# Decoder block: the cross attention of sequence 0 moved into the second self-attention pass, and what moves with it

## The reference

```python
x = x + attn(layernorm(x))            # 16 heads of 128, biases on q, k, v and the output
x = x + xattn(layernorm(x), ctx, ctx) # 8 heads of 64 rows; the q is the sequence's 64x512 row block
x = x + ffn(layernorm(x))             # w2q @ (silu(x w1q) * (x w3q)), 1365 hidden, ternary weights
```

## Time and profile before

| | us |
|---|---|
| median of 3 runs | 1212.6 (1211.21 to 1213.02) |
| the profiled execution, its own time | 1214.28 |
| its span, first to last instruction | 1212.4 |
| PE busy | 1135.5 (94%) |
| DVE, ACT, POOL busy | 755.4, 551.7, 448.4 |

### The profile page before, as it was taken

How to read it: one execution, slowest core, us unless ns; L and a number is a source line. 1 busy time by engine, 2 the same in 40 slices (tenths; PEclk the granted TensorE clock), 3 DMA queues, 4 the chain that set the end, 5 groups by cost and what they waited for, 6 DMA issues and landing times.

```text
span 1212.4 us, 16525 instructions
## 1 busy us (share of the span) xinstructions
PE 1135.5 (94%) x5792; PEld 946.3 (78%) x5792; DVE 755.4 (62%) x1401; ACT 551.7 (46%) x1145; POOL 448.4 (37%) x388
## 2 busy tenths in 40 slices
PE   5999997999999999999999978779998999999997
PEld 3888885878788888888888856568877887888786
DVE  7555459797465655353232478878866886787531
ACT  2455672324151244562332237657727762875230
POOL 2222328041341123380403036546625661674030
PEclk9999999899999999999999979979999999999999
DMA  7455553455302143411200143922203110410000
GB/s 225 132 184 183 188 180 122 162 173 175 110 19 87 52 152 127 148 43 62 70 1 1 44 147 101 309 79 70 62 27 114 61 44 35 122 45 1 35 1 35
DMA packets 52789, 118.99 MB, mean 98 GB/s; under 512 B 9977, under 2 KB 9977, under 8 KB 50666
## 3 DMA queue, kind: packets, MB, share of 16 engines
q1 hardware_dynamic: 52714, 118.03, 30.4%
HBM read 101.22 MB, written 16.79 MB: 97 GB/s over the span
## 4 chain that ended last, share of the span: by engine, by line
PE 80%; DVE 10%; ACT 4%; issue 3%; POOL 2%; DMA 1%; SPq 0%; POOLq 0%; ACTq 0%; DVEq 0%
PE bank L102 16%; PE bank L103 16%; PE bank L104 16%; PE bank L441 6%; PE bank L442 6%; PE bank L405 4%; PE bank L453 3%; PE bank L454 3%; PE bank L415 2%; PE bank L427 2%; PE bank L416 2%; PE bank L428 2%; DVE pxl L615 1%; POOL wal L1415 1%; DVE wlow L1367 1%
## 5 line engine op out<-in xcount | busy, mean ns | idle before, releaser
L441 PE MATMUL bank<-x3h,w 128*128 128x512 f32 (+1 forms) x352 | 141.8, 403 | 1.6 <-DVE x3l L689 1.6
L442 PE MATMUL bank<-x3l,w 128*128 128x512 f32 (+1 forms) x352 | 139.1, 395 | 0.0
L769 POOL TENSOR_SCALAR pe_x<-pe_x,xri,gam 128x512 f32<-128x512 f32 x128 | 101.7, 795 | 100.6 <-DVE xri L624 94.6
L1074 ACT ACTIVATE yh<-bank 128x512 fp32r<-128x512 f32 x64 | 37.9, 601 | 219.8 <-PE bank L104 219.7
L1415 POOL TENSOR_TENSOR wal<-raw_a,wah 128x512 fp32r<-128x512 f32 x44 | 62.3, 1446 | 201.2 <-ACT wah L1095 201.2
L102 PE MATMUL bank<-yh,rh 128*128 128x512 f32 x256 | 101.6, 397 | 10.4 <-DVE xacc L1301 10.4
L535 ACT ACTIVATE pe_x<-bank,xmx 128x512 f32<-128x512 f32 x128 | 88.0, 687 | 40.8 <-DVE xmx L620 39.6
L1232 DVE TENSOR_TENSOR ml<-bank,mh 128x512 fp32r<-128x512 f32 x64 | 43.5, 690 | 100.0 <-ACT mh L1074 100.0
L1420 POOL TENSOR_TENSOR wbl<-raw_b,wbh 128x512 fp32r<-128x512 f32 x64 | 87.8, 1406 | 45.1 <-ACT wbh L1113 45.1
L1232 DVE TENSOR_TENSOR yl<-bank,yh 128x512 fp32r<-128x512 f32 x64 | 43.8, 690 | 96.9 <-ACT yh L1074 96.9
L620 DVE TENSOR_REDUCE xmx<-bank 128x1 f32<-128x512 f32 x128 | 87.3, 682 | 26.5 <-PE bank L416 23.2
(11 more groups left out here) (137 smaller groups left out, 2939.9 us busy)
## 6 DMA issues: line engine op xcount, KB each, us to landing
raw_a<-in_wk SPq DMA_DIRECT2D x8, 1024.0 KB, 5.3
raw_b<-in_wq SPq DMA_DIRECT2D x8, 1024.0 KB, 5.3
raw_a<-in_wo SPq DMA_DIRECT2D x8, 1024.0 KB, 5.5
raw_b<-in_wvt SPq DMA_DIRECT2D x8, 1024.0 KB, 4.9
x1d<-x_scratch SPq DMA_DIRECT2D x64, 128.0 KB, 3.2
kd<-in_ctx SPq DMA_DIRECT2D x64, 128.0 KB, 3.2
ternary_scratch<-wraw SPq DMA_DIRECT2D x24, 341.2 KB, 3.0
w<-ternary_scratch SPq DMA_DIRECT2D x2, 2730.0 KB
```

The costliest lines, as they stand in the source:

```text
L441: pe.matmul(u_bank[w][0:m, :], lhs, x3h[:, c, :], start=c == 0, stop=False)
L442: mm = pe.matmul(u_bank[w][0:m, :], lhs, x3l[:, c, :], start=False, stop=c == CK - 1)
L769: pool.tensor_scalar(pe_x[:, q, :], pe_x[:, q, :], xri[:, q:q + 1], gam[:], ALU.mult, ALU.mult).then_inc(s["xpn"], 1)
```

## The change

Turn 0 is gone. Its 32 steps and the tail of its last head are done inside the second pass: steps between and inside the M tiles of the scores (nine steps for each group of eight tiles, the first of them in the fifth tile of group 0), the tail in the first Y tiles of the values. `early` names a set of tiles for it that lies in memory then free, with one PSUM bank for scores, one for transposes and one for results, where `main` has two, two and one. The M ring has three banks for this part in place of four. The biases of the q weights are added on POOL (`pool_add`) and not on DVE. `xacc` for the second pass is loaded only when the steps are over, since their tiles lie there. The x2 of sequence 0 goes to DRAM and comes back late in the values; its layer norm and transposes lie among the last outputs. W1 is loaded in the values' first group, W3 before the last group, W2 at the start of turn 1. The moments of sequence 3 are formed in the first four steps of turn 1. Turns 1, 2, 3 and the last are all written out, with no loop on any engine.

```diff
+PLACES = (0, 1, 2, 3, 4, 5, 8, 6, 7)
+def early_step(g, place):
+    n = len(PLACES) * g - 4 + PLACES.index(place)
+    return n if n >= 0 else None
...
+        early = Mem(
...
+            s=[bank[6]] * 2, t=[bank[7]] * 2, r=bank[3], ring=1)
...
-        def turns(engine_loop, body):
-            body(0, None, 1)
-            with engine_loop(1, B - 1) as b:
-                body(b, b - 1, b + 1)
-            body(B - 1, B - 2, None)
+        def turns(body):
+            for b in range(1, B):
+                body(b, b - 1, b + 1 if b + 1 < B else None)
             body(None, B - 1, None)
...
+        def sp_w2(sp):
+            sp.wait_ge(s["out_ready"], PASSES * GROUPS * PB * HG)
+            for b in range(B - PB, B):
+                sp.wait_ge(s[f"x1_out{b}"], 16)
...
+        def sp_w13(sp, w):
+            if w == 0:
+                sp.wait_ge(s["a_ready"], A["M", PASSES - 1, GROUPS - 1, CK - 1, PB - 1] + 1)
...
+            else:
+                sp.wait_ge(s["wal_pool"], wal_pool(PASSES, 0))
+                sp.wait_ge(s["wbl"], CK * load(PASSES, 0))
+            sp.dma_start(w13[:, w].bitcast(F32), wq_dram[w].rearrange("(c p) n -> p c n", p=P)).then_inc(s["w_in"], 16)
...
+        def sp_early_start(sp):
+            sp.wait_ge(s["x1_out0"], 16)
+            sp.wait_ge(s["st_out0"], 16)
+            sp_stats(sp, 0)
+            sp_head(sp, early, 0, 0)
+            sp_head(sp, early, 0, 1)
+            sp.dma_start(early.x2[:], x1_dram[0].rearrange("(t p) c -> p t c", p=P)).then_inc(s["x2_in"], 16)
...
+        def sp_early_end(sp):
+            sp.wait_ge(s["r_free"], XH)
+            sp.dma_start(x1_dram[0].rearrange("(t p) c -> p t c", p=P), early.x2[:]).then_inc(s["x2_out"], 16)
...
+        def sp_scores_early(sp):
+            p = PASSES - 1
+            sp_x1_data(sp, p - 1, 0)
+            sp_x1_stat(sp, p - 1, 0)
+            sp_x1_data(sp, p - 1, 1)
+            for g in range(GROUPS):
+                sp_slot_a(sp, p, g + 1)
+                if g + 1 < GROUPS:
+                    sp.wait_ge(s["wadd_b"], wadd_b(p, g + 1))
+                    sp_row(sp, wk, bk, g + 1)
+                if g == 0:
+                    sp_early_start(sp)
+                    sp_slot_b(sp, p, g + 1)
+                    sp_x1_stat(sp, p - 1, 1)
+                    sp_head(sp, early, 0, 2)
+                    sp_head(sp, early, 0, 3)
+                elif g == 1:
+                    sp_head(sp, early, 0, 4)
+                    sp_slot_b(sp, p, g + 1)
+                    sp_head(sp, early, 0, 5)
+                elif g == 2:
+                    sp_head(sp, early, 0, 6)
+                    sp_head(sp, early, 0, 7)
+                    sp_slot_b(sp, p, g + 1)
+                else:
+                    sp_slot_b(sp, p, g + 1)
+                if g + 1 < GROUPS:
+                    sp.wait_ge(s["wadd_a"], wadd_a(p, g + 2))
+                    sp_row(sp, wq, bq, g + 1)
...
+        def pe_t_early(pe, g, pr, before):
+            p = PASSES - 1
+            pe.wait_ge(s["s_read"], pair(p, g, pr) + 1)
+            pe.wait_ge(s["t_free"], before)
...
+        def pe_early_scores(pe, n):
+            h, q = divmod(n, 4)
+            if n == 0:
+                pe.wait_ge(s["out_free"], out_index(PASSES - 2, GROUPS - 1, PB - 1, HG - 1) + 1)
+            pe_sx(pe, early, 0, h, q)
+            if n == 0:
+                pe_vt(pe, early, 0, 0)
+            elif n % 8 == 7 and h + 1 < XH:
+                pe_vt(pe, early, 0, h + 1)
+            if q == 1 and h >= 2:
+                pe_ret(pe, early, 0, h - 2, 1)
+            if q == 3 and h >= 1:
+                pe_ret(pe, early, 0, h - 1, 0)
...
+        def pe_early_turn(pe, n):
+            h, q = divmod(n, 4)
+            if h:
+                pe_pt(pe, early, 0, h - 1, q)
...
+        def pe_scores_early(pe):
+            p = PASSES - 1
+            for g in range(GROUPS):
+                for place in range(2 * CK):
+                    c, i = divmod(place, PB)
+                    n = early_step(g, place)
+                    pe_m_tile(pe, p, g, c, i, range(0, CK // 2))
+                    if n is not None:
+                        if g and place == 4:
+                            pe.wait_ge(s["att_free"], pair(p, g - 1, 0) + 1)
+                        if g and place == 7:
+                            pe.wait_ge(s["att_free"], pair(p, g - 1, 1) + 1)
+                        pe_early_turn(pe, n)
+                    pe_m_tile(pe, p, g, c, i, range(CK // 2, CK))
+                    if n is not None:
+                        pe_early_scores(pe, n)
+                    if place == 3:
+                        pe_s(pe, p, g, 0)
+                        if g:
+                            pe_t_early(pe, g - 1, 0, tiles_before(early_step(g, 4)))
+                    if place == 5:
+                        pe_s(pe, p, g, 1)
+                        pe_early_turn(pe, early_step(g, 8))
+                        pe_early_scores(pe, early_step(g, 8))
+                    if place == 6 and g:
+                        pe_t_early(pe, g - 1, 1, tiles_before(early_step(g, 7)))
+                    if place == 7:
+                        pe_s(pe, p, g, 2)
+                        pe_s(pe, p, g, 3)
...
+        def pe_y_early(pe):
+            last = XH - 1
+            for c in range(CK):
+                pe_y_tile(pe, PASSES - 1, 0, 0, c, range(0, TJ // 2))
+                if c == 0:
...
+                if c == 1:
...
+                pe_y_tile(pe, PASSES - 1, 0, 0, c, range(TJ // 2, TJ))
...
+                act_vt(act, early, 0, h + 1)
+            act_exp(act, early, 0, h, q)
+            if q == 0 and h + 1 < XH:
+                act_prep(act, early, 0, h + 1)
...
+        def act_scores_early(act):
+            p = PASSES - 1
+            for g in range(GROUPS):
+                for place in range(2 * CK):
+                    c, i = divmod(place, PB)
+                    if early_step(g, place) is not None:
+                        act_early_rows(act, early_step(g, place))
+                    act_high(act, mh[:, c % 2, i, :], A["M", p, g, c, i])
+                    if g and 1 <= place <= CK:
+                        act_split_b(act, p, g, [place - 1])
+                    if place == 2 * CK - 1:
+                        act_split_a(act, p, g + 1, range(0, 2))
+                    if early_step(g, place) is not None:
+                        act_early_step(act, early_step(g, place))
+                    if place == 0 and g:
+                        act_attention_half(act, p, g - 1, 1)
+                    if place == 3:
+                        if g:
+                            act_t_half(act, p, g - 1, 0, early.t[0])
+                        else:
+                            act_prep(act, early, 0, 0)
+                    if place == 5:
+                        if g == GROUPS - 1:
+                            act_matrix(act, p, 0)
+                        act_early_rows(act, early_step(g, 8))
+                        act_early_step(act, early_step(g, 8))
+                    if place == 6 and g:
+                        act_t_half(act, p, g - 1, 1, early.t[0])
+                act_split_a(act, p, g + 1, range(2, CK))
+                if g == GROUPS - 1:
+                    act_bias_v(act, p, g + 1)
+                act_attention_half(act, p, g, 0)
...
+        def dve_early_rows(dve, n):
+            h, q = divmod(n, 4)
+            if h:
+                dve_px(dve, early, 0, h - 1, q)
+            if n:
+                dve_rinv(dve, early, 0, (n - 1) // 4, (n - 1) % 4)
...
+        def dve_scores_early(dve, link):
+            p = PASSES - 1
+            for g in range(GROUPS):
+                for place in range(2 * CK):
+                    c, i = divmod(place, PB)
+                    n = early_step(g, place)
+                    if n is not None:
+                        dve_early_rows(dve, n)
+                        dve_early_max(dve, n)
+                    dve_low(dve, ml[:, c % 2, i, :], mh[:, c % 2, i, :], A["M", p, g, c, i])
+                    if n is not None:
+                        dve_early_values(dve, n)
+                    if g == 0 and place < 4:
+                        dve_x1(dve, link, p - 1, 1, place)
+                    if g == 0 and place == 3:
+                        dve_q(dve, early, 0, 0)
+                    if place == 1 and g:
+                        dve_shares(dve, p, g - 1)
+                    if g + 1 < GROUPS:
+                        if place == 2:
+                            dve_row(dve, link, p, g + 1, "a")
+                        if 3 <= place < 3 + CK:
+                            dve_add(dve, p, g + 1, "a", place - 3)
+                        if place == 2 * CK - 1:
+                            dve_row(dve, link, p, g + 1, "b")
+                            dve.sem_inc(s["row_sum"], 1)
+                    elif place == 2 * CK - 1:
+                        dve_bias_v(dve, p, 0)
+                    if place == 5:
```

(32 more changed lines are left out.)

801 lines of the change are left out of this document (487 added, 314 removed).

## The result

Median 1200.4 us (1199.7 to 1203.5, 4 runs) against 1212.8 for the kernel before, a ratio of 0.9907 (0.9893 to 0.9921): 11 us less, or 12.4 by the medians. The forecast was 1183, 29.4 less on the profiled execution's own time. The direction held, and so did the range, whose upper end is 1201, by less than 1 us; more than half of the gain did not come. The profiled execution took 1199.98 us, with a span of 1198.2. All ratios here are of runs in the chip's usual, faster state; the one run outside it (1295.1 us, of the loop alone) is left out.

What follows compares the result with a forecast made beforehand. PE was taken as the bound, unfilled only in turn 0. Removing 97.7 us less 52.8 of replacing work gives 44.9, plus 2.1 for the loop, minus 17.6 of waits: 29.4 less, so 1183 us, range 1170 to 1201.

Steps and rivals of the forecast that it cites:

- rival 3: Clock falls after PE waits near 2.84 us, at the steps' start and turn 1's start: five holes cost 8 us, 1191; chance 0.10.
- (a): First step in group 0 of the second pass's scores: PE waits for DVE, ACT and POOL; net 1.5 us, between 0 and 5.
- (b): Between score groups: `wah` and `wal` come late behind the inserted work; stalls of 5.6 us, between 1 and 12.
- (c): Self-attention transposes share the one transpose bank: PE waits for ACT's copy 0.5 us six times, 3 in all, 0 to 6.
- (d): Layer norm of sequence 0 on DVE before the first of the last outputs: PE waits about 1.5 us, 0 to 4.
- (e): Tail of the moved work in the Y tiles: 1 us of waits, 0 to 3.
- (f): Moments of sequence 3 in turn 1's first four steps delay DVE's maxima and the exponentials: 5 us, between 2 and 8.
- The loop: Turn 2 written out instead of entered over the loop's back edge should be like turn 3: 2.1 us gained.
- Rival 1: Everything fits: waits of 5 us in all in place of 17.6, giving 1171; chance 0.12.
- Rival 2: The single score bank binds: 1.1 us more for each of 32 steps, giving 1208; chance 0.11.
- Rival 4: DVE operations lose time to POOL on the shared port: 12 us more at a whole POOL operation each, 1195; chance 0.06.
- Rival 5: Bias rows come late to DVE six times in the second pass: at 7 us late each, 1225; chance 0.06.

Runs made afterwards that it cites:

- the filled waits: Changed kernel with matmuls nobody reads put into three PE waits (16 before the first step, 11 before the third output, 12 before the last turn's first `pe_down`): 1194.9 us, 0.9868.
- the three tries: Changed kernel with first-step loads reordered: two heads' context first, 1199.7 us; head 0's only, DVE's subtraction ahead of sequence 1's chain, 1209.4; same, chain in idle stretches, 1196.5.
- the second try: Changed kernel with only head 0's context loaded first, its rows right behind the statistics, DVE's subtraction ahead of sequence 1's chain: 1209.4 us, 0.9969.

## Why the prediction was wrong

The mechanism was right: turn 0 is gone, PE goes from the last output into sequence 1, turns 1 to 3 last what was forecast. What failed is the size of "what the new arrangement costs" and of "what takes its place on PE", and the clock, which the sum had at nothing: 15.7 us in one stage, 7.4 of waits, 4.7 of clock and 3.6 of work. That the range held, with 1200.4 against its end of 1201, is luck: it allowed waits of up to 34 us and no clock.

1. **The clock (rival 3), at nothing in the sum.** 4.7 us. I gave the mechanism a chance of 0.10 and 8 us, and kept it out of the sum, though the earlier trace rows show it behind a wait of 2.84 and my own terms made waits near that length. Shown by PE's busy time in the stage with the clock at 1.00 (365.0, and 365.2 with the filled waits, not 369.7) and by the 4.7 us that the filled waits gave, of which some 1.5 belong to the last turn. Of the two places that the rival named, the first step had the fall and turn 1's start had not.
2. **(a), the first step.** 4.1 of wait, not 2.9. I followed DVE's list and took the loads as landed. They were late: the 128 KB loads, four of each factor, took a median of 6.5 us to land there (396 to 412 us), with the DMA engines at a share of 1.06 to 1.12 from 400 to 408 us, and 3.0 to 3.1 in turn 2 at a share of 0.22. ACT's copy of the query came when forecast (408.15), but POOL still had the other factor to do and began 1.1 us late. The chain on DVE ended at the same time as the loads, and both had to go to shorten the wait (the three tries). Of the 1.4 that I set against it, 0.5 was misread: the earlier trace rows are of the whole span, and the second wait at this place is 0.31.
3. **(b), between groups.** 4.1 for `wal` and 1.1 for `ml`, against 5.6: right in sum. By group it is 1.4, 1.1, 2.7 and nothing, against 2.0, 0.8, 1.8 and 1.0. **(c)**, the transposes: 2.8 against 3, but in three waits, two of them of 1.3, not in six of 0.5.
4. **(d), the layer norm of sequence 0.** 2.6, not 1.5, and the clock behind it. This was the dearest single place, 7.5 us with what the clock gave back elsewhere.
5. **(e), the tail.** 2.5 (1.4 and 1.1), not 1. The 1.1 is a result's addition. The 1.4 is not: with the addition of head 6 out of the way 1.25 of it stayed. It is for ACT's copy of a transpose, which stands behind four exponentials of the self attention (579.10 to 580.57).
6. **Not foreseen.** 2.9 for the value transposes, which wait for DVE's low part of the head before, behind ACT's exponentials; 1.3 for the single score bank. The value transposes are in no term, since I listed waits by what a step needs and left out what the shared bank's tile before it needs.
7. **PE's own work: 48 was 3.6 short.** 53.2 of busy time at full clock, against 49.6. I had taken 0.1 for each of 32 breaks. From the starts of the matmuls in the profile with the earlier layer norm, the inserted pieces take 44.9 (44.5 forecast), and the neighbours of the pieces 3.3 more than elsewhere: both right. What is missing stands at the edges of the waits, 3.0 us at 22 matmuls beside one (0.6 before). The last matmul ahead of a wait counts as busy for 0.39 us and not for the 0.23 to the next start, and the first one behind starts its neighbour later (411.16 to 411.46). Some 1.4 more are spread over matmuls with no break near them, and for those I have no cause.
8. **(f), turn 1.** 1.48, 1.68 and 1.22 in waits and a turn of 117.3: right in number. But the edit that took the moments away took 3.9 of these waits and brought 2.0 at 808 to 810, so it won 1.4. That the moments alone cost the 5 us is not borne out; in part this number is luck.
9. **The loop.** 2.1 seen in turn 2, not in the time: by itself 0.4, at most 1.5.

Rival 1 fell with waits of 21.4 us in the stage. Rival 2 fell: only 1.3 us of waits hang on the single score bank. The single transpose bank is dearer, 7.1 us (2.9, 2.8 and 1.4), of which the sum had 3 in (c) and a part in (e). Rival 4 can't be told from the list of waits, as it makes DVE's operations longer. They are: from 392 to 530 us DVE's operations took 8.4 us more than the shortest of their kind (3.7 in the scores before), and the pairs of `wal` 2.38, 3.25 and 3.47, where the pair took 1.28 at 448.06 before: up to 1.1 an operation, between the 0.6 of the row and a whole POOL operation. So a part of the 4.1 for `wal` may be the port; no run takes POOL's work away. Rival 5 did not happen in the changed kernel (DVE waits 0.40 for the row at 428.45), but the second try made it happen, and PE went on 6.4 us later than in the changed kernel (436.49, not 430.12) for one row that was issued 4.3 us late.

Open: whether the 3.0 for the shares and 4.2 for `wal` that are left can go as well. No order was tried for them.

## What to carry to other kernels

When work is threaded into a full engine, list for every inserted piece which engine's queue stands before its releaser, and give the longer waits (here 2 to 4 us) a price for the slower matmuls that can follow; here the clock was almost a third of the missing gain. An edit that shortens one wait is measured best with the clock held in the others, or its gain can't be told from theirs, and a table of waits says what is the edit's own. And before a producer is moved later, look at what stands behind its store in the queue that issues transfers: a store that waited 16 us longer held back loads that had nothing to do with it.
